# Gelu of six feed-forwards read from three score banks, in one group, with the order planned for it

## The reference

```
def block(x, context, ...):
    h1 = _ln(x, n1_g, n1_b)
    x = _attn(h1, h1, q1, k1, v1, o1_w, o1_b, 20) + x
    h2 = _ln(x, n2_g, n2_b)
    x = _attn(h2, context, q2, k2, v2, o2_w, o2_b, 20) + x
    h3 = _ln(x, n3_g, n3_b)
    proj = h3 @ ff_w1 + ff_b1
    a, g = jnp.split(proj, 2, axis=-1)
    ff = a * jax.nn.gelu(g, approximate=False) @ ff_w2 + ff_b2
    return ff + x
```

## Time and profile before

| | |
|---|---|
| median of 3 runs | 889.87 us (886.49 to 891.96) |
| the profiled execution | 890.55 us, span 888.8 us |
| mean granted TensorE clock | 0.994 |
| TensorE busy | 846.8 us (95%) |
| VectorE busy | 690.5 us (78%) |
| ScalarE busy | 650.8 us (73%) |
| GpSimd busy | 57.6 us (6%) |

### The profile page before, as it was taken

One profiled execution on the slowest core, in us unless ns is written; L12 is line 12 of the kernel. 1 busy time (PEld: TensorE's weight loads), 2 busy tenths in 40 slices (PEclk: granted clock), 3 DMA queues, 4 the chain that ended last, 5 costly groups with the idle time before them and its releaser, 6 DMA issues.

```text
span 888.8 us, 19864 instructions
## 1 busy us (share of the span) xinstructions
PE 846.8 (95%) x7796; PEld 564.4 (64%) x7796; DVE 690.5 (78%) x1653; ACT 650.8 (73%) x1415; POOL 57.6 (6%) x98
## 2 busy tenths in 40 slices
PE   8999999999999999999999999999989999999986
PEld 6556556566766665766667666566567655666555
DVE  4888888877878888777777657777698898877853
ACT  8677786877776878677786677577867788867661
POOL 2000010000100000000001000000000000010010
PEclk9999999999999999999999999999999999999999
DMA  4621221111111111110000200002201121111100
GB/s 107 188 49 25 68 66 25 32 24 31 27 36 37 37 25 37 25 40 13 22 2 1 79 1 2 23 3 61 57 20 34 37 49 37 25 25 37 40 1 15
DMA packets 26964, 32.45 MB, mean 37 GB/s; under 512 B 9332, under 2 KB 17912, under 8 KB 26872
## 3 DMA queue, kind: packets, MB, share of 16 engines
q1 hardware_dynamic: 26872, 31.19, 13.9%
HBM read 9.54 MB, written 0.66 MB: 11 GB/s over the span
## 4 chain that ended last, share of the span: by engine, by line
PE 77%; DVE 12%; ACT 8%; issue 2%; POOL 0%; DVEq 0%; ACTq 0%
PE pv_ps L1091 17%; PE bank_ps L1031 13%; PE bank_ps L1051 12%; DVE mx L1519 7%; PE bank_ps L1134 5%; PE bank_ps L1250 4%; PE bank_ps L1012 4%; ACT probs L1341 4%; PE bank_ps L1013 4%; PE bank_ps L1065 4%; PE bank_ps L1116 4%; PE bank_ps L1215 3%; PE bank_ps L1261 3%; PE bank_ps L1202 2%; ACT oT L1350 1%
## 5 line engine op out<-in xcount | busy, mean ns | idle before, releaser
L1519 DVE TENSOR_REDUCE mx<-bank_ps 128x1 f32<-128x512 f32 (+3 forms) x720 | 450.9, 683 | 68.9 <-PE bank_ps L1051 67.0
L1341 ACT ACTIVATE probs<-bank_ps 128x512 f32<-128x512 f32 x736 | 380.8, 603 | 89.8 <-PE bank_ps L1031 87.7
L1091 PE MATMUL pv_ps<-probs,v_all 128*9 128x256 f32 (+2 forms) x2944 | 201.9, 379 | 4.0 <-ACT probs L1341 1.9
L1031 PE MATMUL bank_ps<-qT,ring 64*128 64x256 f32 x1280 | 171.0, 304 | 2.5 <-DVE qT L1543 0.8
L1031 PEld LDWEIGHTS bank_ps<-qT,ring 64*128 64x128 f32 x1280 | 127.4, 185 | 62.8 <-issue 17.8
L1051 PE MATMUL bank_ps<-ring,qT 64*128 64x512 f32 (+1 forms) x800 | 165.2, 395 | 1.1 <-DVE qT L1543 0.6
L1051 PEld LDWEIGHTS bank_ps<-ring,qT 64*128 64x128 f32 x800 | 86.7, 185 | 49.9 <-issue 25.6
L1091 PEld LDWEIGHTS pv_ps<-probs,v_all 128*9 128x9 f32 (+2 forms) x2944 | 57.8, 91 | 76.8 <-issue 25.4
L1392 ACT ACTIVATE kdense<-bank_ps 128x512 fp32r<-128x512 f32 (+2 forms) x116 | 58.5, 555 | 26.4 <-PE bank_ps L1134 25.9
L1543 DVE TENSOR_TENSOR qT<-bank_ps,qT 128x256 fp32r<-128x256 f32 (+1 forms) x108 | 47.3, 438 | 27.8 <-PE bank_ps L1065 27.7
L1321 ACT ACTIVATE ks<-bank_ps 128x320 fp32r<-128x320 f32 x80 | 36.6, 459 | 36.9 <-PE bank_ps L1013 22.0
(11 more groups left out here) (185 smaller groups left out, 987.0 us busy)
## 6 DMA issues: line engine op xcount, KB each, us to landing
ring<-kdense SPq DMA_DIRECT2D x240, 64.0 KB, 2.0
ring<-kdense SPq DMA_DIRECT2D x160, 32.0 KB, 1.9
gate<-in_w_up SPq DMA_DIRECT2D x4, 640.0 KB, 4.2
wb<-in_w_blk SPq DMA_DIRECT2D x2, 960.0 KB, 5.1
wd<-in_w_down SPq DMA_DIRECT2D x2, 400.0 KB, 5.4
x<-in_x SPq DMA_DIRECT2D x4, 160.0 KB, 4.3
bias<-in_bias SPq DMA_DIRECT2D x1, 640.0 KB
out_rows<-x SPq DMA_DIRECT2D x4, 160.0 KB, 2.1
```

Source lines behind the costliest of these rows:

```text
L1031: mm = pe.matmul(bank[0:kr, i * a["nq"]:(i + 1) * a["nq"]], key_op(n, h)[:, c * P:c * P + kr], query_rows(u, b, h), start=True, stop=True)
L1091: mm = pe.matmul(pv_ps[32 * j:32 * j + a["dh"] + 1, 0:a["nq"]], v, probs[0:kr, s % N_P, i * a["nq"]:(i + 1) * a["nq"]], start=(c == 0), st ...
L1341: nc.scalar.activation(probs[0:kr, s % N_P, 0:w], bank[0:kr, 0:w], ACT.Exp, scale=float(a["dh"]) ** -0.5).then_inc(free, 1)
L1519: nc.vector.tensor_reduce(mx[b][0:rows, t, heads[0]:heads[-1] + 1:heads[-1] - heads[0] or 1], bank[0:rows, 0:a["hpm"] * a["nk"]].rearrange ...
```

## The change

The six feed-forwards no longer have an Identity eviction. Their `ff_g` is TensorE's part alone, and `gelu` takes Gelu with bias from the three banks, in five instructions of 256 columns, freeing each bank as it is read. `ff_a` on VectorE waits for its own gate bank to be taken, not for all. The semaphore `gate_ready` is gone. The planner is told of it: `ff_g` has no price on ScalarE and its bank stays taken until `gelu` is done, and `gelu` is priced at 2560 ns and five chunks.

```diff
--- before.py
+++ after.py
@@ -349,6 +349,8 @@
         return n * TR, dve(4 * n, 32 * n, LINK)
     if kind in ("ff_g", "ff_a"):
         n = min(2, FC - 2 * step[3])
+        if kind == "ff_g" and step[1:3] not in LAST_FEEDS:
+            return n * 4 * 107, []
         return n * 4 * 107, (act if kind == "ff_g" else dve)(*n * [SQ])
     return {
         "ctx_tr": (4 * TR, act(32, 512)), "kv_proj": (f32(320), act(320, 160)),
@@ -357,7 +359,7 @@
         "o_proj": (f32(640), dve(320)), "ln": (0, [("dve", 760), ("pool", 910)]), "norm": (0, dve(200, 200) if step[1] not in ("ff1", "ff3") else dve(160, 160, 160, 160, 128)),
         "w_in": (0, [("dma", 3000)]), "w_high": (0, act(FC * SQ)), "w_low": (0, dve(FC * SQ)),
         "x_bias": (0, [("pool", 821)]), "x_keys": (0, act(640, 320) + dve(320)),
-        "gelu": (0, [("act", 3700)]), "ff_o": (f32(10 * D), dve(320)), "ca_q": (f32(160), act(320)),
+        "gelu": (0, [("act", 2560)] + act(*FC * [SQ])), "ff_o": (f32(10 * D), dve(320)), "ca_q": (f32(160), act(320)),
         "ca_kv": (350, dve(32, 32, 160)), "c_tr": (2 * TR, act(96, 96)), "c_q": (f32(4 * 96), act(96, 96)),
         "c_s": (f32(64), dve(32, 32) + act(32)), "c_norm": (0, dve(32, 8, 32)), "c_p": (f32(256), act(256)), "c_o": (f32(512), dve(256, 256)),
         "store": (0, []),
@@ -601,7 +603,8 @@
             if step[0] in LOW:
                 self.low.append(("low", step))
             if bank is not None:
-                self.banks[bank] = ("low", step) if step[0] in LOW else step
+                gelu = step[0] == "ff_g" and step[1:3] not in LAST_FEEDS
+                self.banks[bank] = ("low", step) if step[0] in LOW else ("gelu", *step[1:3]) if gelu else step
 
         def worth(self, choice, horizon, others):
 
@@ -669,7 +672,7 @@
     "negm_ready": {"negm"},
     "out_full": {"pv_last"}, "out_taken": {"oev"}, "k_high": {"kv_proj", "x_keys", "qkv_proj"}, "x_split": {"x_keys"},
     "q_high": {"q_proj", "ca_q"}, "f_high": {"f_tr"}, "up_high": {"w_high"}, "up_ready": {"w_low"}, "x_biased": {"x_bias"}, "var_ready": {"ln"},
-    "rstd_ready": {"ln"}, "xn_ready": {"norm"}, "gate_ready": {"gelu"}, "c_exp": {"c_s"}, "c_probs": {"c_norm"},
+    "rstd_ready": {"ln"}, "xn_ready": {"norm"}, "c_exp": {"c_s"}, "c_probs": {"c_norm"},
 }
 
 
@@ -1319,6 +1322,15 @@
                     n = (t1 - t0) * (D // dh)
                     v = src.rearrange("p (h d) -> p h d", d=dh).unsqueeze(2).broadcast_to([rows, n, 2, dh])
                     return nc.scalar.activation(out, v, ACT.Copy)
+
+                def gelu_of(step):
+
+                    _, tag, b, i = step
+                    bank, free = filled(act, step)
+                    for k, m in enumerate(range(2 * i, min(2 * i + 2, FC))):
+                        c = (0 if tag == "ff1" else 2 * FC) + FC + m
+                        ins = nc.scalar.activation(gate_of(tag, b)[:, m, :], bank[:, k * SQ:(k + 1) * SQ], ACT.Gelu, bias=cols[:, c:c + 1])
+                    ins.then_inc(free, 1)
 
                 act.wait_ge(s_warm, 1)
                 half_rows = slice(64, P)
@@ -1439,19 +1451,11 @@
                             n = min(2, ATT[u]["H"] // of(u) - 2 * gg)
                             dst, w = query_op(u, b)[:, 2 * gg:2 * gg + n, :].rearrange("p g q -> p (g q)"), n * SQ
                         nc.scalar.activation(dst, bank[:, 0:w], ACT.Copy).then_inc(free, 1)
-                    elif kind == "ff_g":
-                        _, tag, b, i = step
-                        bank, free = filled(act, step)
-                        for k, m in enumerate(range(2 * i, min(2 * i + 2, FC))):
-                            c = (0 if tag == "ff1" else 2 * FC) + FC + m
-                            ins = nc.scalar.activation(gate_of(tag, b)[:, m, :], bank[:, k * SQ:(k + 1) * SQ],
-                                                       ACT.Gelu if (tag, b) in LAST_FEEDS else ACT.Identity, bias=cols[:, c:c + 1])
-                        ins.then_inc(free, 1)
+                    elif kind == "ff_g" and step[1:3] in LAST_FEEDS:
+                        gelu_of(step)
                     elif kind == "gelu":
-                        _, tag, b = step
-                        for i in (1, 2):
-                            taken(act, ("ff_g", tag, b, i))
-                        nc.scalar.activation(gate[:, :, :], gate[:, :, :], ACT.Gelu).then_inc(S["gate_ready"], 1)
+                        for i in range(3):
+                            gelu_of(("ff_g", *step[1:], i))
                     elif kind == "c_s":
                         taken(act, step)
                         nc.scalar.activation(cs[:, :], cs[:, :], ACT.Exp, scale=20.0 ** -0.5).then_inc(S["c_exp"], 1)
@@ -1622,10 +1626,7 @@
                     elif kind == "ff_a":
                         _, tag, b, i = step
                         bank, done = filled(dve, step)
-                        if (tag, b) in LAST_FEEDS:
-                            taken(dve, ("ff_g", tag, b, i))
-                        else:
-                            dve.wait_ge(S["gate_ready"], value["gate_ready", ("gelu", tag, b)])
+                        taken(dve, ("ff_g", tag, b, i))
                         for k, m in enumerate(range(2 * i, min(2 * i + 2, FC))):
                             c = (0 if tag == "ff1" else 2 * FC) + m
                             g = gate_of(tag, b)[:, m, :]
```

## The result

| | before | after |
|---|---|---|
| median, runs | 890.91 us of 4 (886.49 to 892.29) | 898.77 us of 4 (897.56 to 901.14) |
| profiled execution | 890.55 us, span 888.8 | 898.9 us, span 897.1 |
| mean granted TensorE clock | 0.994 | 0.994 |

The ratio is 1.0096, with a 95% interval of 1.0073 to 1.012: the changed kernel is about 8 us slower. The range of 881 to 900 held that; the predicted 890.0 lies 8.8 us off. In one of the experiments (label k1_order_only) the profiled execution was disturbed (1270.08 us, mean granted clock 0.556), so that kernel is read from its three other runs, and there is no trace of it to compare.

The account below looks back on a forecast made before the run. TensorE was taken as the bound, busy 846.8 of 888.8 us, with ScalarE 238 us slack. Terms -1.3 + 2.0 + 0.7 - 2.4 + 1.3 gave +0.3 us on the 889.87 median: 890 us, range 881 to 900.

Parts of the forecast that it names:

- ScalarE's work: All six Gelu groups: six 1280-column Gelus go, 7.6 us less of 650.8; loads stay 14; stretch without Exp 4.61 us.
- First group, +2.0: Gelu group near 351 us: TensorE waits 1.1 us for a held bank and 1.1 for a later Exp; +2.0 us.
- Third group, -1.3: Gelu group near 451 us: the chain runs through ScalarE's loads and Gelu, so the saving counts in full; -1.3 us.
- rival A: First, third, fourth groups: TensorE starves and its clock drops; +10 us, 900 us; 0.21 together with an unlucky order.
- Second, fourth and sixth, -0.8 each: Groups near 403, 490 and 807 us: waits paced by VectorE's maxima shrink in the new order; -2.4 us together.
- Fifth, +0.7: Gelu group near 773 us: TensorE waits for a bank that VectorE's maxima free; +0.7 us.
- The order itself, +1.3: Everything from step 1219 on, planned anew: 11 more changes of matmul kind at 0.12 us; +1.3, between 0 and +4.7.
- The 8 to 9 us that I gave the draw of a new order: From about 345 us on: uncertainty of a new order, from idle spread over ten stretches; forecast band 881 to 899, chance 0.62.
- Rival B: All six groups: ScalarE's queue sets the pace, so 7.6 us and 2.3 idle go; 880 us; 0.17 with a lucky order.

Follow-up runs that it names:

- k1_order_only: The changed kernel's order with the old work (Identity evictions, one Gelu over 1280 columns): ratio 1.0103, median of three runs 898.6 us.
- k3_two_direct: Before, in its own order, with only groups four and six taking Gelu straight from the banks, directly behind the last gate tile: 891.43 us, ratio 1.0008.
- k_price: The changed kernel with the planner's price of its Gelu step set to 4520 ns instead of 2560 plus five chunks: 899.17 us, ratio 1.0112.
- 3690 to 3830: Before with the planner's old Gelu price at 3690, 3700 (before itself), 3710 and 3830 ns: 887.48, 890.91, 885.06 and 898.89 us.
- the run at 2550: The changed kernel with the loads in its Gelu step priced 2550 instead of 2560 ns: 888.69 us, ratio 0.9969.
- k2_gelu_up: The changed kernel with each Gelu group moved directly behind its last gate tile, TensorE's order kept: 894.76 us, ratio 1.0066.
- k_up_2550: The changed kernel priced at 2550 ns, with each Gelu group moved directly behind its last gate tile: 890.01 us, ratio 0.9993.

## Why the prediction came out as it did

*ScalarE's work: right.* 643.7 us where 643 was predicted. The Gelus from the bank take 1.93 us in a row of five instead of the 2.05 that I took from the Identities, and 476 ns on average. The loads stay 14 (seven and six in the rows of after, and one at the start). The stretch is 4.5 us where 4.61 was said. The bank's Gelu begins 1.29 us after the load (347.16 to 348.45), so the drain that the Trainium skill adds to a load (ScalarE: Activation LUTs, What ACT_TABLE_LOAD costs) is not seen in after either.

*First group, +2.0: right in mechanism and nearly in size.* I had walked it to two waits of 1.1 us, for the bank that the Gelu frees and for the fourth Exp behind the load back. The trace has 0.53 and 1.04 for these, and 0.58 for a maximum that I had not walked to: 2.15 together. The window around it has 2.0 us more idle time than before. One reading under it was wrong: the chain of before is not TensorE's throughout this group, it has six maxima of VectorE (344.45 to 348.14) between the first eight and the other twelve gate matmuls; TensorE idles only 0.13 us in the 20 from 345, so the term is not touched.

*Third group, -1.3: wrong.* I let the saved Gelu count in full because the chain of before ran there over the load. In the new order this group has the row of twenty and the Exp in front of the load as well; the chain is ScalarE's from 448.93 to 454.70, TensorE stands still 0.17 + 0.59 + 1.41 us between 451 and 455, and the clock falls. I had walked the first group's order and not this one's, though rival A named the place.

*Second, fourth and sixth, -0.8 each: not borne out.* In the sixth the maxima in the chain are 3.69 us instead of 4.29, 0.6 less, as said, but from the first gate matmul to the other half it is 8.33 us (812.61 to 820.94) instead of 7.67, with three score tiles for Exp (0.23 each) more between them: no gain is left. In the second the chain went over to ScalarE, and TensorE's idle time stayed as it was. And in the order of before the same work in groups four and six is worth between -0.6 and +2.1 us together (k3_two_direct), not -1.6. The bound that I gave for it, held banks costing what they cost in the first group (+2.0 each), is not reached either; the sixth group shows +0.6. *Fifth, +0.7:* the wait for maxima that I walked to is there (3.69 us in the chain, none before); its size alone was not measured.

*The order itself, +1.3: this is the step that failed.* "The sum fails most easily on the new order away from the groups, which I priced only by its changes of kind." Measured with old work, the new order costs 1.03% of 890, which is +9.2 us (+6.6 to +11.8), far outside the bounds 0 to +4.7. Changes of matmul kind are no measure of an order: k_price has 728 of them and is the slowest, before 736. The 8 to 9 us that I gave the draw of a new order as its spread kept the result within the range: four draws with old work, 3690 to 3830, lie between 885.1 and 898.9 us. That it fits is partly luck, as it is the 4 us out of ten stretches doubled without a number for the doubling, and the result lies only 0.2 us inside the 899 that it gives and 1.2 inside the range.

*Rival A (900 us): its mechanism occurred once, and its time is right for another reason.* One of the three groups it named lost the clock: 3.4 us at the lower level (2 x 2 us x 0.44, and x 0.41), which costs at most 1.7, after waits of 0.59 and 1.41 us rather than the 1.7 in one piece that I took as the point from which it decides. No run shows such a point: the same wait of 1.34 us was followed by a fall once and once not. Nor was that example the only fall in the trace of before (it is at 0.72 in 36 to 42 too). By the move of the Gelu this place is worth about 3 us in this order. But held banks do not explain the total, as k1_order_only frees them early and takes 898.6 us all the same (the median of its three runs). *Rival B (880 us)* is out: ScalarE lost the time and the chain did not shorten.

*What stays open.* Why 2560 draws a worse order than 2550. The two differ from step 1515 on, and most of the difference is made from 445 to 645 us. Between 344 and 848 us after has one wait of over 2 us, 2.30 for a maximum, ending at 641.51, with the clock at 0.74 and 0.83 in the two windows of 4 us from 640; the run at 2550 has none over 1.39. No single wait was isolated by a run. Of k1_order_only there is no comparable trace, so where its time goes was not seen, only that it is the same amount. How much of it the clock's falls cost, beside the waits ahead of them, was not tried: no run here changes the one without the other. And the orders were all planned for one Gelu price or another; new work in all six groups of the order of before was not run.

## What to carry to other kernels

Where a planner or scheduler orders the work, an edit of its prices is two changes, the work and a new order, and the second can be the larger: here 10 ns in one price moved a kernel whose TensorE is busy 95% by up to 1.3%. Hold the order fixed and change the work, or run old and new work over several orders, before saying what the work is worth. And since orders can be drawn by the dozen by moving a price by 10 ns, running a few and keeping the fastest (885.06 us here) won more than the edit did.

## What the runs showed of the hardware

A Gelu with bias over 256 columns from a bank took 0.386 us in a row of five (1.93 us at the first and the third group), slightly less than the Identity's 0.41; nothing in before showed a row of such Gelus.

The clock fell behind shorter waits than the one example of before: the two of 0.59 and 1.41 us at the third group, with matmuls between them, came just before the window at 0.56. The Trainium skill has activity release the clock (TensorE: Matmul & The Clock Gate, What's actually happening), and the falls here behind pauses agree. But such waits do not decide alone: with the same steps and the same wait of 1.34 us the clock stayed at 1.00 in k2_gelu_up and went to 0.60 in k_up_2550. During and behind the wait of 4.30 us in k_price the clock was at 0.64 and then at 0.50 in windows of 4 us.
